# Raw dt computed twice on ScalarE instead of once on VectorE

## The reference, cut to what matters

```
bcd = x_ @ x_proj_w                        # 16 B columns, 16 C columns, one dt column
dt  = softplus(bcd[..., -1:] * dt_w + dt_b)   # one number per row and channel
dA  = exp(dt[..., None] * A)               # 16 states
h   = dA_t * h + (dt * x_)_t * B_t ;  y_t = sum_n h * C_t     # 32 steps in time
```

## Time and profile before

| | us |
|---|---|
| median of three runs | 2110.63 |
| the profiled execution's own time | 2108.97 |
| its span, first to last instruction | 2107.2 |
| TensorE matmuls busy | 1938.8 (92%) |
| VectorE busy | 1846.9 (88%) |
| ScalarE busy | 1681.0 (80%) |
| GpSimd busy | 465.5 (22%) |

### The profile page before, as it was taken

The page is one execution under the profiler, slowest core; times in us unless marked ns, Lnnn a source line. Parts: engine busy times, 40 slices in busy tenths (PEclk is TensorE's granted clock), DMA queues, the critical chain, the costliest instruction groups (busy, mean ns, idle before and its releaser), DMA issues.

```text
span 2107.2 us, 37698 instructions
## 1 busy us (share of the span) xinstructions
PE 1938.8 (92%) x11723; PEld 1376.6 (65%) x11738; DVE 1846.9 (88%) x2311; ACT 1681.0 (80%) x4617; POOL 465.5 (22%) x395
## 2 busy tenths in 40 slices
PE   6999899999999999999999999999999999567799
PEld 4667676666767666676676666767676676456444
DVE  1544899999999999999999999999999999988678
ACT  2447888888888889898888888888889898656584
POOL 1000222221313132131312222313132231200013
PEclk9999999999999999999999999999999999789899
DMA  7722332333333333343332333333333232410214
GB/s 209 277 83 66 69 101 70 71 91 75 96 81 97 74 98 73 83 96 85 85 96 68 73 88 80 90 81 100 71 98 81 83 83 74 120 41 11 71 40 140
DMA packets 93163, 187.95 MB, mean 89 GB/s; under 512 B 18736, under 2 KB 39872, under 8 KB 87872
## 3 DMA queue, kind: packets, MB, share of 16 engines
q1 hardware_dynamic: 78448, 133.32, 20.0%
q0 software_dynamic: 14544, 52.96, 13.2%
HBM read 116.12 MB, written 17.18 MB: 63 GB/s over the span
## 4 chain that ended last, share of the span: by engine, by line
PE 38%; issue 18%; ACT 17%; DVE 13%; DVEq 1%; ACTq 0%; POOL 0%; POOLq 0%
ACT dA L1348 8%; PE bank L918 7%; PE bank L927 6%; PE bank L1017 5%; PE bank L1057 5%; DVE xs L1631 3%; PE bank L1119 3%; PE bank L1141 3%; PE bank L964 2%; ACT Pr L1242 2%; DVE hb L1690 2%; PE bank L998 2%; PE bank L955 2%; DVE hb L1695 2%; PE bank L1082 1%
## 5 line engine op out<-in xcount | busy, mean ns | idle before, releaser
L1348 ACT ACTIVATE dA<-dt,A_sb 128x124 f32<-128x124 f32 x2048 | 615.0, 390 | 17.6 <-DVE dt L1645 16.2
L1695 DVE TENSOR_TENSOR_SCAN hb<-dA,hb 128x2048 f32<-128x2048 f32 x116 | 513.2, 4424 | 24.8 <-ACT dA L1348 20.3
L927 PE MATMUL bank<-wv_sb,ctxT 128*128 128x512 f32 x1024 | 472.5, 605 | 0.9 <-ACT ctxT L1175 0.9
L918 PE MATMUL bank<-ctxT,wk_sb 128*128 128x256 f32 x2048 | 458.3, 382 | 4.3 <-ACT ctxT L1175 4.3
L918 PEld LDWEIGHTS bank<-ctxT,wk_sb 128*128 128x128 f32 x2048 | 383.7, 190 | 63.1 <-ACT ctxT L1175 7.8
L927 PEld LDWEIGHTS bank<-wv_sb,ctxT 128*128 128x128 f32 x1024 | 192.8, 196 | 201.1 <-issue 199.0
L1442 POOL DMA_DIRECT2D hb<-hb x101 | 91.6, 907 | 905.2 <-DVE hb L1701 893.7
L1690 DVE TENSOR_TENSOR hb<-u,BC 128x2048 f32<-128x2048 f32 x116 | 265.8, 2291 | 5.6 <-DVE u L1657 2.6
L1701 DVE TENSOR_TENSOR hb<-hb,BC 128x2048 f32<-128x2048 f32 x115 | 264.0, 2296 | 1.5
L1017 PE MATMUL bank<-xn2T,win_sb 128*128 128x128 f32 x2048 | 235.4, 276 | 0.8 <-ACT xn2T L1267 0.7
L1017 PEld LDWEIGHTS bank<-xn2T,win_sb 128*128 128x128 f32 x2048 | 232.3, 192 | 3.6 <-ACT xn2T L1267 1.3
(11 more groups left out here) (156 smaller groups left out, 2635.0 us busy)
## 6 DMA issues: line engine op xcount, KB each, us to landing
hb<-hb POOLq DMA_DIRECT2D x101, 512.0 KB, 4.6
ctx_sb<-in_ctx_dram SPq DMA_DIRECT2D x64, 512.0 KB, 3.6
BC<-bcd_dram SPq DMA_DIRECT2D x32, 1024.0 KB, 6.3
maskb<-in_mask_Bx1x1xS_fk_dram SPq DMA_DIRECT2D x64, 128.5 KB, 3.2
wstage<-in_L_ffn_w_dram SPq DMA_DIRECT2D x4, 2048.0 KB, 11.0
x_sb<-in_x_dram SPq DMA_DIRECT2D x16, 256.0 KB, 3.3
win_sb<-in_L_attn_in_proj_w_dram SPq DMA_DIRECT2D x1, 4096.0 KB, 25.1
bo_sb<-bias_dram SPq DMA_DIRECT2D x64, 64.0 KB, 2.0
```

Of the source, the lines that this page charges most:

```text
L918: last = pe.matmul(bank[6 + j][:, (m % 2) * KF:(m % 2 + 1) * KF], wk_sb[:, c, m * P:(m + 1) * P], ctxT[:, c, :], start=(c == 0), stop=(c = ...
L927: last = pe.matmul(bank[h][:], ctxT[:, c, h * P:(h + 1) * P], wv_sb[:, c, :], start=(c == 0), stop=(c == DC - 1))
L1348: last = act.activation(dA[:, c % 2, n * BT:(n + 1) * BT, 1:], dt[:, c, :].rearrange("p (b s) -> p b s", s=S)[:, :, 1:], ACT.Exp, scale=A_ ...
L1695: ins = dve.tensor_tensor_scan(flat, dA[:, c % 2].rearrange("p n s -> p (n s)"), flat, 0.0, ALU.mult, ALU.add)
```

## The change

VectorE's eight instructions for raw dt are gone, and so is ScalarE's one Abs over all chunks. Instead ScalarE takes the copied row itself, eight times with Abs (into `soft_tmp`) and eight times with Relu (into `dt`), each with `dt_w` as the per-partition scale and `dt_b` as the per-partition bias. Exp and Ln follow as before. VectorE's merge becomes a plain addition of the two. The places of the remaining steps are the same; the counts of the semaphores follow.

```
-            part.mamba_steps(LAST)          # in tail; likewise in interval, b == 2

 def dt_row (ScalarE):
-    wait(act, dt_step, 10 * t)
+    wait(act, dt_act, 5 * t)

 def mamba_softplus (ScalarE):
-    act.wait_ge(dt_step, 10 * t + 8)
-    act.activation(soft_tmp, dt[:], ACT.Abs).then_inc(dt_act, 1)
-    act.wait_ge(dt_act, 4 * t + 1)
+    act.wait_ge(dtrow_copied, t + 1)
+    act.wait_ge(conv_done, (TAPS - 1) * IC * (t + 1))
+    for c in range(IC):
+        last = act.activation(soft_tmp[:, c, :], BC[:, 2 * NS, :], ACT.Abs, scale=chan[:, 1, c:c + 1],
+                              bias=chan[:, 2, c:c + 1])
+    last.then_inc(dt_act, 1)
+    wait(act, u_ready, 2 * t)
+    wait(act, dA_ready, IC * t)
+    for c in range(IC):
+        last = act.activation(dt[:, c, :], BC[:, 2 * NS, :], ACT.Relu, scale=chan[:, 1, c:c + 1],
+                              bias=chan[:, 2, c:c + 1])
+    last.then_inc(dt_act, 1)
+    act.wait_ge(dt_act, 5 * t + 1)
     act.activation(soft_tmp, soft_tmp, ACT.Exp, scale=-1.0).then_inc(dt_act, 1)
-    act.wait_ge(dt_act, 4 * t + 2)
+    act.wait_ge(dt_act, 5 * t + 3)
     (Ln in two halves, as before)

-def mamba_steps (VectorE):
-    dve.wait_ge(dtrow_copied, t + 1)
-    wait(dve, dA_ready, IC * t)
-    for c in range(IC):
-        dve.tensor_scalar(dt[:, c, :], BC[:, 2 * NS, :], chan[:, 1, c:c + 1], chan[:, 2, c:c + 1],
-                          ALU.mult, ALU.add).then_inc(dt_step, 1)

 def mamba_dt (VectorE), for each half:
-    dve.wait_ge(dt_act, 4 * t + 3 + i)
-    dve.scalar_tensor_tensor(dt half, dt half, 0.0, soft_tmp half, ALU.max, ALU.add).then_inc(dt_step, 1)
+    dve.wait_ge(dt_act, 5 * t + 4 + i)
+    dve.tensor_tensor(dt half, dt half, soft_tmp half, ALU.add).then_inc(dt_step, 1)
```

More of the change, by code:

```diff
@@ L631, in dt_row @@
             def dt_row(self, t, keys): pass
-            def mamba_steps(self, t): pass
             def mamba_softplus(self, t): pass
@@ L1271, in mamba_pad @@
                     if q == 0:
-                        wait(act, dt_step, 10 * t)
+                        wait(act, dt_step, 2 * t)
                     act.wait_ge(in_psum, 4 * t + q + 1)
@@ L1338, in decays @@
                         if half == 0:
-                            act.wait_ge(dt_step, 10 * t + (9 if c < IC // 2 else 10))
+                            act.wait_ge(dt_step, 2 * t + (1 if c < IC // 2 else 2))
                             if isinstance(t, int) and (t == LAST or t == PREV and c >= 6):
@@ L1448, in mamba_pad @@
                         return
-                    wait(pool, dt_step, 10 * t)
+                    wait(pool, dt_step, 2 * t)
                     apart(pool)
@@ L1631, in mamba_conv @@
                                 dve.scalar_tensor_tensor(acc, src, tap, acc, ALU.mult, ALU.add).then_inc(conv_done, 1)
-                def mamba_steps(self, t):
-                    dve.wait_ge(dtrow_copied, t + 1)
-                    wait(dve, dA_ready, IC * t)
-                    for c in range(IC):
-                        dve.tensor_scalar(dt[:, c, :], BC[:, 2 * NS, :], chan[:, 1, c:c + 1], chan[:, 2, c:c + 1],
-                                          ALU.mult, ALU.add).then_inc(dt_step, 1)
                 def mamba_dt(self, t):
                     for i, half in enumerate((slice(0, IC // 2), slice(IC // 2, IC))):
-                        dve.wait_ge(dt_act, 4 * t + 3 + i)
-                        dve.scalar_tensor_tensor(dt[:, half, :], dt[:, half, :], 0.0, soft_tmp[:, half, :],
-                                                 ALU.max, ALU.add).then_inc(dt_step, 1)
+                        dve.wait_ge(dt_act, 5 * t + 4 + i)
+                        dve.tensor_tensor(dt[:, half, :], dt[:, half, :], soft_tmp[:, half, :], ALU.add).then_inc(dt_step, 1)
                 def mamba_u(self, t):
@@ L1654, in mamba_u @@
                     for i, half in enumerate((slice(0, IC // 2), slice(IC // 2, IC))):
-                        dve.wait_ge(dt_step, 10 * t + 9 + i)
+                        dve.wait_ge(dt_step, 2 * t + 1 + i)
                         dve.wait_ge(xs_ready, t + 1)
```

1 line of the change is left out of this document (removed).

## The result

The changed kernel takes 2151.76 us (median of four runs, 2151.5 to 2152.55) against 2109.89 for the kernel before (four runs beside it, 2108.9 to 2110.73): 41.9 us slower, ratio 1.020, 95% interval 1.0184 to 1.0217. I had forecast 2161 us and a range of 2132 to 2184.

The account below looks back on a forecast made before the run. Bound: order of waits among locked engines, with VectorE's merge awaiting ScalarE's softplus in b = 2. Sum: 49.4 (tiles 1 to 13) + 5.0 + 2 - 5.8 = +50.6 us, forecast 2161 us, range 2132 to 2184.

Parts of the forecast that it names:

- The place and the mechanism: Half b = 2: ScalarE's longer softplus makes VectorE's merge +5.0 us late, VectorE idle about 7 us, TensorE +1.9.
- The spacing of the activations: ScalarE's sixteen new instructions start every 0.39 us (ends 0.29 and 0.483), +5.15 us on ScalarE before Exp.
- The cover: VectorE's 1.18 us wait for decays later in the period absorbs part of the delay, leaving +3.8 a period.
- tile 14's own 5.0: In tile 14's interval VectorE no longer waits for decays at this place, so nothing covers: +5.0 us.
- The first tile: Existing waits of VectorE and ScalarE take in part of the 5.0 us, leaving +2 (0 to +4).
- The tail: Last tile: without raw-dt steps waiting 5.82 us for the previous tile's decays, the merge comes 5.8 us earlier.
- The clock's fall in TensorE's new wait: TensorE's longer wait for L964 in b = 2 may lower its clock; counted at nothing, +0.5 us a period as bound.
- rows 6: Earlier trace's rows showing VectorE's 1.18 us wait for decays at 1248.80, the only wait a delay can eat.
- (a): Rival, each period: delay not absorbed at all, 5.0 us on each of 14 tiles, +66 us, 2177; chance 0.14 with more.
- (b): Rival, ScalarE's new activations: spacing near 0.29, +25 us, 2135; chance 0.15, shared with a larger cover.
- (c): Rival: VectorE's work is the bound, its 2.0 us come back in 14 tiles plus the tail, -34 us, 2077; chance 0.04.
- (d): Rival: TensorE is the real bound and the 5.0 us vanish in slack, 2108 to 2113 us; chance 0.03.

Follow-up runs that it names:

- after_early: Changed kernel with ScalarE's order in b = 2 altered: Abs and Relu before the second key copies, Exp and Ln before the scaling; 2104.29 us, ratio 0.997 to the kernel before.
- spread: Kernel before plus twelve idle ScalarE activations, four each in front of three places where ScalarE waits; 2119.33 us, ratio 1.006.
- block_before: Kernel before plus twelve idle ScalarE activations put ahead of the softplus in tiles 0 to 14; 2183.5 us, ratio 1.037.
- steps_out: Kernel before without VectorE's eight raw-dt instructions, Abs and merge reading the convolution's output instead; 2100.8 us, ratio 0.997.
- abs_only: Kernel before, VectorE's steps kept, with the one Abs replaced by eight Abs from the copied row; 2123.5 us, ratio 1.008.
- tail_only: Kernel before with the changed softplus in the last tile alone; 2103.41 us, ratio 0.998.
- exp_direct: Changed kernel with softplus as ln(1 + exp(r)) on ScalarE, without Abs, Relu or VectorE's merge; 2100.23 us, ratio 0.996 to the kernel before.
- block_behind: Kernel before plus twelve idle ScalarE activations behind the Ln and ahead of the decays; 2161.27 us, ratio 1.026.
- before_sooner: Kernel before with the second half of chunk 2's decays moved ahead of ScalarE's key copies and scaling in b = 3; 2101.65 us, ratio 0.995.

## Why the prediction was right, point by point
**The place and the mechanism.** The forecast was that VectorE's merge, not ScalarE's busy share, carries the cost. The merge did come 5.00 us late against the reciprocal (+5.0 forecast), and VectorE's wait there is 6.9 us (7 forecast). TensorE's products came 15.0 us after the reciprocal instead of 13.11, +1.9 as forecast. after_early took most of the loss away without taking any work away, and spread placed 6 us of work at a sixth of the price.

**The spacing of the activations.** 0.385 us against 0.39 taken. Inferring from two shapes (the strided tap and the long ln_out) that each per-partition operand costs about 0.1 us held: the second one costs 0.084, 0.484 against the 0.400 of the earlier trace rows. The lower end, 0.29, would have been wrong. The Trainium skill states this rule, in "ScalarE: Activation LUTs", section "What ACT_TABLE_LOAD costs": 186 ns plus 0.833 a column, 93 for each such operand, and back-to-back instructions overlap by 93. The estimate worked out from it is 0.386 us a piece, and the trace after agrees with 0.385. The idle activations on 32 partitions in block_before did not overlap; they start every 0.50 us.

**The cover.** This term was mis-sized. I had 1.18 us a period; 1.75 were covered. The scan's wait gave its 1.18. The gap before the first scores of the interval, in which VectorE waits for nothing that the profile shows, fell from 0.75 to 0.38; it did so in steps_out too, and stayed 0.75 in abs_only, so it goes with the eight removed instructions. And the 0.20 us before u shrank to 0.03. Thus 5.00 - 1.75 = +3.25 in the period that the timelines show, +3.3 on average of the twelve, where the sum had 3.8.

**What the cover is made of.** The prediction took the 1.18 us as room that is simply there. The periods that lack it point to TensorE's slower clock as its source. In the profiled execution of the kernel before the clock falls behind the wait in b = 1 in ten of the twelve periods. In the other two, those of tiles 5 and 12, it stays up (granted 1.00 from 850 to 854), and the next scan of b = 3 waits for nothing:

```profile
849.58 1.96 PE L955 MATMUL bank<-idf,Pr 128*128 128x128 f32 x8 [1.62 <-ACT Pr L1242]
...
909.98 4.42 DVE L1695 TENSOR_TENSOR_SCAN hb<-dA,hb 128x2048 f32<-128x2048 f32 x1
```

The period of tile 6 takes 111.65 us, not 112.7. tail_only, whose periods are those of the kernel before, has three such cases (111.39, 111.68 and 111.69 us). In the 26 periods of the two traces, from the merge of tile 1 to that of tile 14, the wait of 1.1 to 1.2 us stands in every one behind a fall and in none of the five behind b = 1 at full clock. The changed kernel hardly feels the falls, since its VectorE comes later anyway (115.8 and 116.0 us behind periods without one, 116.05 otherwise). Against 111.65 the delay of 5.00 costs 4.4 us, and only the 0.57 us of the other two gaps are covered. That the cover of 1.18 held is thus due to a fall that the prediction had read the earlier trace rows but had not connected with the earlier trace rows. No run sets the clock by itself, so this rests on the periods that differ in it. The first row also corrects a reading: the prediction charged the clock with the 1.5 us by which the eight transposes take longer than in b = 2 (2.53 against 1.04), but at full clock they take 1.96 there, so the clock's part is 0.57.

**The ends.** Tile 13 has +4.55 (114.5 us to the merge of tile 14, against 110.0), where I had 3.8; tile 14's own 5.0 is the first term of the sum below. The 110.0 us belong to one execution: the period stands behind a b = 1 without a fall. In tail_only the same instructions stand behind a fall, the scan waits its 1.18 us, and the period takes 111.34; against that it is +3.2, like the others. The first tile: the merge 3.7 us late, but with 1.3 us won before the change's first instruction (the first dt row is copied at 187.2 instead of 188.5, which is not the change's doing), so 5.0; of this 1.25 is carried on, where I had +2. The tail: -5.5 for -5.8.

**The sum.** 5.0 + 1.25 + 39.8 + 4.55 at the merge of tile 14 is 50.6, less 5.5 in the tail, 1.3 at the start and 0.4 behind: 43.4 us of span, for 50.6 forecast. The cover makes 12 x 0.5 = 6 of the 7 us between them. The clock's fall in TensorE's new wait, which I had kept as a bound only, came in two of the twelve periods, in those of tiles 1 and 3 (granted 0.66 from 323 to 328). They take 116.19 and 115.81 us, so it is worth nothing in the sum. TensorE's wait in b = 1 did not shrink either, as I had thought it might: it is still 1.60 us. The forecast came out 7 us too high, inside the range; every term was within 0.8 us of what it measured, so no large errors cancelled. Luck had a part in the cover: the sum took rows 6 for every period, and the fall behind it came in nearly every one.

**The rivals.** (a), nothing absorbed, and (b), cheap activations, are out by the 1.75 and the 0.385. (c), VectorE as the bound, is refuted by steps_out and exp_direct: 2.0 and 3.3 us a tile taken from it shorten the period by only 0.1. (d) is out by the result.

## What to carry to other kernels
Between engines that meet several times a period, work has no price of its own; it has one where it stands. Before moving work, find the next instruction of another engine that needs its result, take the time from the last common event to it on both engines, and compare; then look whether the step could stand earlier in its engine's order, since a step that has lost an input (here the softplus its raw dt) may start sooner, and in this case that turned 42 us lost into 5 gained, about 10 of them by TensorE's clock. Time saved on a busy engine is a gain only if nobody is waited for next. And before you count a wait as room for a delay, look in the periods where it is missing: here it came and went with the clock of a third engine.

## What the runs showed of the hardware
- Twelve activations of 128 columns on 32 partitions each, with two per-partition operands, last 0.487 us each and start every 0.50; sixteen on 128 partitions last 0.485 and start every 0.385. So the twelve did not overlap. What prevents it was not tried; each of the twelve reads and writes another group of partitions than the one before it.
- VectorE's gap at the edge of the loop, with no wait in it, is 0.75 us with the eight raw-dt instructions in the loop, 0.38 without, and 0.15 in the interval behind the loop.
- The length of TensorE's wait alone does not tell whether its clock falls to 1.2 GHz. Behind the wait in b = 1 it falls in ten of twelve periods of the kernel before and in two of twelve of after_early, and nearly all of these waits are 1.61 to 1.63 us long. In block_behind it held behind the waits of 2.15 us and fell in each of the seven periods with one of 3.4.
- A period with a fall in b = 1 is 1.0 us longer in after_early; in the kernel before the one behind it is 1.0 to 1.1 us longer, and in the changed kernel at most 0.25.
- VectorE's product by C in b = 0 takes 2.29 us where GpSimd's addition has ended before it starts, and up to 3.22 in before_sooner, where the addition runs beside it.
